# The convolution's banded product as 64x64 tiles on TensorE, its zero quarters left out, each half of the contraction in PSUM banks of its own

## The reference

```python
# first layer: per-batch mixing of the 64 channels, then a binary-weight product
x = x + _L0_ffn_ref(_L0_cond_ref(x, cond_128, ...), ...)
# second layer: a grouped convolution along the 1024 positions, then a product with W, Wq, Wk, A, Bm
def _L1_cond_ref(x, c, weight, c_weight, bias):
    C_OUT, K, GROUPS = (64, 9, 4)
    out = lax.conv_general_dilated(x, weight, window_strides=(1,), padding=[(4, 4)],
                                   dimension_numbers=('NCH', 'OIH', 'NCH'), feature_group_count=GROUPS)
    ctx = jnp.einsum('nd,od->no', c, c_weight)
    return out + ctx[:, :, None] + bias[None, :, None]
def _L1_ffn_ref(x, W, b, Wq, Wk, A, Bm):
    result = jnp.einsum('bsi,oi->bso', x, W) + b
    q, k = x @ Wq.T, x @ Wk.T                      # 8 experts of 32 each, here in short
    w = jax.nn.softmax((q * k).sum(-1) / math.sqrt(32), axis=-1)
    h = jnp.einsum('bsi,eri->bser', x, A)
    return result + jnp.einsum('bse,bser,eor->bso', w, h, Bm)
x = x + _L1_ffn_ref(_L1_cond_ref(x, cond_128, L1_cond_weight, L1_cond_c_weight, fside_S_0), L1_ffn_W, ...)
```

## Time and profile before

| what | value |
|---|---|
| median of 3 runs | 585.76 us (585.52 to 588.63) |
| the profiled execution | 585.94 us |
| its span | 584.2 us |
| TensorE, matmul records | 569.8 us busy (98% of the span), x3381 |
| VectorE | 232.6 us (40%) |
| ScalarE | 118.9 us (20%) |
| GpSimd | 148.1 us (25%) |
| DMA | 58.16 MB, mean 100 GB/s |
| chain that ended last | PE 94% |
| of it, line 473 (the convolution) | 10% |

### The profile page before, as it was taken

One profiled execution on the slowest core, in us unless ns is written; L12 is line 12 of the kernel. 1 busy time (PEld: TensorE's weight loads), 2 busy tenths in 40 slices (PEclk: granted clock), 3 DMA queues, 4 the chain that ended last, 5 costly groups with the idle time before them and its releaser, 6 DMA issues.

```text
span 584.2 us, 9131 instructions
## 1 busy us (share of the span) xinstructions
PE 569.8 (98%) x3381; PEld 502.3 (86%) x3381; DVE 232.6 (40%) x446; ACT 118.9 (20%) x271; POOL 148.1 (25%) x79
## 2 busy tenths in 40 slices
PE   4799999999999999999999999999999999999997
PEld 3688888888888899989989889899899898898996
DVE  3675677557765555221232232222312322222121
ACT  4732333324233341011111011011110110100100
POOL 0425636555456456101011011011010110110100
PEclk9889999999999999999999999999999999999999
DMA  8905324443253664303203123033032130230100
GB/s 327 356 34 162 117 78 132 135 119 117 76 175 100 158 165 123 111 3 113 90 24 112 45 67 112 33 79 103 9 112 75 37 112 36 76 111 8 67 37 36
DMA packets 36175, 58.16 MB, mean 100 GB/s; under 512 B 4097, under 2 KB 24385, under 8 KB 36161
## 3 DMA queue, kind: packets, MB, share of 16 engines
q1 hardware_dynamic: 36016, 57.70, 31.9%
q10 hardware_dynamic: 144, 0.26, 0.1%
HBM read 41.15 MB, written 16.79 MB: 99 GB/s over the span
## 4 chain that ended last, share of the span: by engine, by line
PE 94%; DVE 0%; issue 0%
PE bank L491 49%; PE bank L429 21%; PE bank L473 10%; PE bank L391 4%; PE bank L382 4%; PE bank L519 4%; PE bank L405 1%; PE bank L397 0%; PE bank L512 0%; PE bank L411 0%; DVE work L748 0%; DVE work L874 0%
## 5 line engine op out<-in xcount | busy, mean ns | idle before, releaser
L491 PE MATMUL bank<-early,parts 128*128 128x320 f32 (+1 forms) x1152 | 206.5, 337 | 0.0
L491 PEld LDWEIGHTS bank<-early,parts 128*128 128x128 f32 x1152 | 184.7, 188 | 15.7
L429 PE MATMUL bank<-late,parts 128*128 128x512 f32 x512 | 134.5, 411 | 1.5 <-ACT parts L609 1.5
L429 PEld LDWEIGHTS bank<-late,parts 128*128 128x128 f32 x512 | 93.5, 193 | 21.9 <-ACT parts L609 1.9
L931 POOL TENSOR_TENSOR work<-work,bias_bc 128x1024 f32<-128x1024 f32 x16 | 38.7, 2424 | 286.5 <-DMA work<-x_scratch 286.5
L491 PE MATMUL bank<-late,parts 128*128 128x512 f32 x384 | 94.2, 394 | 0.0
L491 PEld LDWEIGHTS bank<-late,parts 128*128 128x128 f32 x384 | 70.9, 188 | 16.1
L473 PE MATMUL bank<-band,raw 128*128 128x128 f32 x512 | 59.7, 275 | 0.0
L473 PEld LDWEIGHTS bank<-band,raw 128*128 128x128 f32 x512 | 59.0, 192 | 0.1
L609 ACT ACTIVATE parts<-work 128x512 fp32r<-128x512 f32 x64 | 39.8, 632 | 80.3 <-DVE work L823 43.0
L899 POOL TENSOR_TENSOR work<-work 128x512 f32<-128x512 f32 x32 | 41.3, 1291 | 52.5 <-DVE work L784 52.5
(11 more groups left out here) (88 smaller groups left out, 344.4 us busy)
## 6 DMA issues: line engine op xcount, KB each, us to landing
xs<-in_x SPq DMA_DIRECT2D x16, 512.0 KB, 3.9
x_scratch<-work SPq DMA_DIRECT2D x16, 512.0 KB, 3.0
raw<-x_scratch SPq DMA_DIRECT2D x128, 64.0 KB, 3.0
work<-x_scratch SPq DMA_DIRECT2D x16, 512.0 KB, 3.6
out_tokens<-work SPq DMA_DIRECT2D x15, 512.0 KB, 2.7
stage<-in_wearly SPq DMA_DIRECT2D x8, 576.0 KB, 3.8
row_bc<-token_rows_scratch SPq DMA_DIRECT2D x30, 64.0 KB, 3.6
work<-in_wsign SPq DMA_DIRECT2D x3, 512.0 KB, 11.3
```

What stands on the lines that cost most here:

```text
L429: last = mm(bank[4 + h][:, :], parts[:, p, a, c, :], signs[:, c, h * HALF:(h + 1) * HALF], start=(k % 16 == 0), stop=(k % 16 == 15))
L491: return mm(dst, parts[:, p, a, c, :], w(b, c), start=(k == 0), stop=(close and k == 23))
```

## The change

Each convolution is cut into products with 64 partitions of contraction and 64 stationary columns (64 output partitions). Of the four quarters of the band (half of the rows by half of the moving columns) one is zero in each step, and is left out: the low rows with s = 1 and the high rows with s = 0 meet all 128 moving columns, the low rows with s = 0 the first 64 alone, and the high rows with s = 1 the last 64 alone (`steps` below). The low rows add into banks 0 and 1, the high rows into two banks `other`: 2 and 3 for the first convolution, else those of the output of the tile whose turn is next. VectorE adds the two.

Since those banks are read by the sums of L874 (L897 in the new text), TensorE waits for `out_ready` before the convolution and not only before the period that writes them. The waits for `raw_loaded` and `out_ready` stand in front of the 37th of the 48 products.

```diff
-            def product_conv(i, p):
+            def inputs_of_conv(i, p):
                 pe.wait_ge(raw_loaded[p], (i + 1) * (16 * L8))
+
+            def product_conv(p, other):
+                low, high = slice(0, S), slice(S, P)
+                steps = ((low, 1, slice(0, P)), (high, 0, slice(0, P)), (low, 0, low), (high, 1, high))
                 for n in range(NBG):
-                    for s in range(2):
-                        last = mm(bank[n // 4][:, (n % 4) * P:(n % 4 + 1) * P], raw[:, p, n, s:s + P],
-                                  band[:, s * GROUPS + n % 4, :], start=(s == 0), stop=(s == 1))
-                    if n % 4 == 3:
-                        last.then_inc(conv_done, 1)
+                    for k, (rows, s, cols) in enumerate(steps):
+                        into = (bank[n // 4], bank[other + n // 4])[k % 2]
+                        at = (n % 4) * P
+                        for g in range(2):
+                            last = mm(into[g * S:(g + 1) * S, at + cols.start:at + cols.stop],
+                                      raw[rows, p, n, s + g * S:s + (g + 1) * S],
+                                      band[rows, s * GROUPS + n % 4, cols], start=(k < 2), stop=(k >= 2))
+                        if n % 4 == 3 and k >= 2:
+                            last.then_inc(conv_done, 1)
...
+                        if h == 1 and k == 12 and ni is not None:
+                            inputs_of_conv(ni, q)
+                            if late_ready:
+                                pe.wait_ge(out_scale_ready, 2 * TILES)
+                            else:
+                                pe.wait_ge(out_ready, 4 * i + 2 * p)
...
                 if ni is not None:
-                    product_conv(ni, q)
+                    product_conv(q, 4 + 2 * q)
...
-            def add_context(i, p, halves=(0, 1)):
+            def add_context(i, p, other, halves=(0, 1)):
...
-                    dve.wait_ge(conv_done, 4 * i + 2 * p + h + 1)
-                    v.tensor_tensor(zt, bank[h][:, :].rearrange("p (n l c) -> p n l c", n=4, l=L8),
-                                    add.broadcast_to([P, 4, L8, CG]), ALU.add).then_inc(z_biased, 1)
+                    dve.wait_ge(conv_done, 8 * i + 4 * p + 2 * h + 1)
+                    v.tensor_tensor(zt, by_group(bank[h]), add.broadcast_to([P, 4, L8, CG]),
+                                    ALU.add).then_inc(conv_halved, 1)
+                    dve.wait_ge(conv_done, 8 * i + 4 * p + 2 * h + 2)
+                    dve.wait_ge(conv_halved, 4 * i + 2 * p + h + 1)
+                    v.tensor_tensor(zt, by_group(bank[other + h]), zt, ALU.add).then_inc(z_biased, 1)
```

More of the change, by code:

```diff
@@ L187, in adaln_ffn_kernel @@
         conv_done = sem("conv_done")
+        conv_halved = sem("conv_halved")
         z_biased = sem("z_biased")
@@ L484, in _ @@
                     pe.wait_ge(pads_zeroed, 2)
-                    product_conv(0, 0)
+                    pe.wait_ge(u_ready, 2 * TILES)
+                    inputs_of_conv(0, 0)
+                    product_conv(0, 2)
                 ffn0_step(last_i, 1, k)
@@ L502, in period1 @@
                 if ni is not None:
-                    product_conv(ni, q)
+                    product_conv(q, 4 + 2 * q)
                 if late_ready:
                     pe.wait_ge(scaled, 2 * TILES)
-                    pe.wait_ge(out_scale_ready, 2 * TILES)
                 o = [bank[4 + 2 * p], bank[5 + 2 * p]]
@@ L812, in _ @@
             period0(last, 0, last, 1, False)
-            def add_context(i, p, halves=(0, 1)):
+            def add_context(i, p, other, halves=(0, 1)):
                 dve.wait_ge(ctx_loaded[p], 16 * (i + 1))
                 dve.wait_ge(z_lo, 4 * i + 2 * p)
+                by_group = lambda made: made[:, :].rearrange("p (n l c) -> p n l c", n=4, l=L8)
                 for h in halves:
-                    dve.wait_ge(conv_done, 4 * i + 2 * p + h + 1)
                     zt = y_t[:, :, 64 * h:64 * h + 64].rearrange("p l (n c) -> p n l c", c=CG)
                     add = row_bc[:, p:p + 1, 64 * h:64 * h + 64].rearrange("p l (n c) -> p n l c", c=CG)
-                    v.tensor_tensor(zt, bank[h][:, :].rearrange("p (n l c) -> p n l c", n=4, l=L8),
-                                    add.broadcast_to([P, 4, L8, CG]), ALU.add).then_inc(z_biased, 1)
+                    dve.wait_ge(conv_done, 8 * i + 4 * p + 2 * h + 1)
[4 more added lines that the diff above has]
+                    v.tensor_tensor(zt, by_group(bank[other + h]), zt, ALU.add).then_inc(z_biased, 1)
             dve.wait_ge(u_lo, 2 * TILES)
-            add_context(0, 0)
+            add_context(0, 0, 2)
             take_rest(0, 0, z_hi, z_lo, by_token)
@@ L861, in period1 @@
                 if ni is not None:
-                    add_context(ni, q, (0,))
+                    add_context(ni, q, 4 + 2 * q, (0,))
                 dve.wait_ge(wh_hi, t1)
@@ L867, in period1 @@
                     take_rest(ni, q, z_hi, z_lo, by_token, (0,))
-                    add_context(ni, q, (1,))
+                    add_context(ni, q, 4 + 2 * q, (1,))
                     take_rest(ni, q, z_hi, z_lo, by_token, (1,))
```

## The result

The change takes 578.89 us (median of 4 runs, 578.03 to 579.43) against 585.64 us for the kernel before on the same chip (585.13 to 588.63, 4 runs); the ratio is 0.9874, 95% interval 0.9844 to 0.9904. That is 1.0 to 1.6% faster. The forecast was 591.3 us, slower than before, and so had the wrong sign, though its wide range (576 to 612) holds the measured time. What was measured is near the first rival, four tiles by themselves (577 us).

What follows compares the result with a forecast made beforehand. TensorE's chain was taken as the bound: loads and streams 3.57 us plus entry and exit 0.35 make 3.92 against 3.57 us, +0.35 a convolution, x 16 = +5.6 us: 591.3 us. Range 576 to 612 us, the forecast's own 585 to 595.

Steps and rivals of the forecast that it cites:

- the first rival: Convolution: column halves load and stream independently, 3.02 us each, 8.8 us less in all, 577 us; chance 0.26.
- What bounds the kernel: Whole kernel: TensorE's gapless chain bounds it; the convolution's 16 x 3.57 = 57.1 us count fully in the time.
- The streams: Convolution: moving columns cost 0.334 us a block if four tiles run side by side, against 0.446 before.
- What runs side by side: TensorE: row groups run side by side and pass one another; for two column halves of one row group the trace shows nothing.
- The weight loads: Convolution: a row group's eight loads of 0.056 us go one behind another, 0.446 us a block, same as before.
- Entry and exit: Around each convolution: going from whole array to tiles and back costs 0.35 us, paid sixteen times.
- VectorE and the moved waits: VectorE's 22 us of added sums are hidden, and the moved waits for `out_ready` and `raw` cost nothing.
- The rival of strict order: Convolution: records keep program order over all tiles, 0.67 to 0.70 us a block, 620 to 624 us; shared chance 0.17.
- Column halves in line: Convolution: column halves run one after another, 5.7 us each, 34 us more in all, 620 us; shared chance 0.17.
- the middle variant: Convolution: tiles side by side but in order within a row group, 3.5 us, 585 to 586 us; chance within the forecast's 0.47.
- The sequencer: Convolution: issuing 128 records and loads is the bound if a pair costs over 0.028 us; with mixtures 596 to 612, chance 0.10.

Runs made afterwards that it cites:

- e7: The changed kernel with the convolution cut in two in the 15 second-stage periods, first four blocks behind the 37th of 48 products: 584.02 us, ratio 0.9936.
- e1: The changed kernel with the zero quarters multiplied too, so all eight products of a block have 128 moving columns: 591.95 us, ratio 1.0083.
- e3: The kernel before with only its stationary columns in two halves (128 rows, whole band, no second banks or sum): 590.27 us, ratio 1.0054.
- b1: The changed kernel with the first-stage router products' stationary columns also in two tiles of 64: 570.08 us in one execution.
- e8: The changed kernel without VectorE's second sum, leaving out half of the convolution's result: 579.41 us, ratio 0.9864.
- e5: The changed kernel reordered: in each convolution half all 32 records of the low rows, then the 32 of the high rows: 605.65 us, one execution.
- e6: The changed kernel reordered: in each convolution half all 32 records of the first 64 stationary columns, then the other 64: 605.44 us, one execution.
- the router's quarters: The changed kernel with the first-stage router products' stationary columns also in four tiles of 32: 571.27 us, ratio 0.9733.
- row halves alone: The changed kernel with row halves and zero quarters left out, but the stationary columns not halved: 592.38 us, ratio 1.0106.

## Why the prediction was wrong, step by step

**What bounds the kernel: right.** The chain is TensorE's, and the change moved the time by what it moved there. (The granted clock was full from the fourth slice on, not from the third; nothing hangs on it.)

**The streams: right.** 0.334 us a block for four tiles side by side were predicted, and 0.334 to 0.335 were measured (e7). The two terms are a little off in opposite ways: 0.112 and 0.055 us were taken for the wide and the narrow record, e1 gives (3.65 - 0.17)/32 = 0.109 for the wide one, which leaves 0.058 for the narrow one. That they cancel is luck.

**What runs side by side: half used.** The prediction read in the earlier trace rows that row groups pass one another, and left open whether two column halves in one row group do. They do, with whole rows (e3) as with half rows. The second record of a float32 product waits for its tile, but the other tiles' records pass it.

**The weight loads: the step that failed.** "If the two column halves of a row group load one behind the other, that is 8 x 0.056 = 0.446 us a block ... I take 0.446." They load side by side: in the change four loads begin together and the next four 0.06 us later, in e3 two and two, and a block takes 0.334 us. The price of a load was right (0.054 us for 64 columns by b1, 0.056 estimated), the number of them that queue was doubled. The choice went by line 391, which has one load after another because all of them are the whole array wide. It says what a load costs and nothing of how many go at once. The same trace had loads of two row groups side by side in line 405, at the same distance as one, and was as near a row. This step alone makes 0.90 us a convolution, 14.4 us: 591.3 less 14.4 is 576.9, against the measured 578.9.

**Entry and exit: right.** 0.35 us were predicted. The chain shows the way back by itself, 0.18 us; with a second entry (e7) it is 0.16 in and 0.20 back, 0.36 together. Of the streams' gain of 0.90 us a convolution this takes two fifths.

**VectorE and the moved waits: right.** Nothing for either (e8, and no wait of TensorE in the second stage).

**The rivals.** The first gave 3.02 us a convolution, 577 us; measured are 2.84 + 0.18 = 3.02 and 578.9 us. It had a chance of 0.26. The Trainium skill's page TensorEngine Tiling (Array Packing), section Key Properties of Tiling Modes, says the same of different tiles, that they can load and multiply in parallel; the four records and four loads that begin together agree. The rival of strict order falls by the same rows and by the some 7 records that TensorE passes over in e5 and e6. The Trainium skill's page TensorE: Matmul & The Clock Gate, Part 3, states that matmuls start and end strictly in program order, and that a load overlaps running matmuls only where its row group differs. This case's runs differ from both, and decide: a later record starts first in e5, and in e3 two loads begin within 0.02 us although all of them take all rows. The page speaks of a load beside a running matmul and not of two loads in a queue, so the forecast did not follow from it either. Column halves in line would have been 5.7 us a convolution, and the middle variant 3.5; both are far from 3.02. The sequencer isn't the bound at 0.021 us a record, the rate of the change: the router's quarters ran 64 records in 0.65 us, 0.010 each.

The sum for the change is 16 x 0.545 = 8.7 us; the medians differ by 6.75, and the interval of the ratio gives 5.6 to 9.1. In the profiled execution 1.5 us went in the first 40 us; why is not shown.

## What to carry to other kernels

A product that is smaller than the array, or whose matrix has zero blocks, can be cut into tiles that load and multiply at the same time, if entry and exit (0.36 us around the convolution) are paid once for many records and if the order in the code changes tiles within some eight records. Which cut pays depends on the limit: moving columns are saved by leaving out zero blocks, but only if the loads are halved too (row halves alone gained nothing), and a product that is limited by its loads gains by column tiles alone, without extra banks or sums. And a row that shows the price of one thing at a time doesn't say that two of them queue: where only that decides, give both cases equal weight and look for a row in which two were offered at once.

## What the runs showed of the hardware

- Four records, as many as there are tiles, began within 0.03 us, and each tile was limited by its own work: 0.109 us for a float32 record of 128 moving columns (e1), about 0.058 for 64 (the change, less that).
- A load cost about its width: 0.106 us for 128 columns, 0.054 for 64, 0.030 for 32 (with 8 moving columns, 0.17 us taken off for the entry to tiles), and loads of different column tiles went side by side.
- TensorE passed over some 6 to 8 waiting records to start one whose tile was free, across row halves and across column halves alike.
- From the whole array to tiles and back cost 0.36 us around the convolution, of which about half lay in the products behind; behind the router's column tiles these took only 0.08 us more.
- 64 loads and 64 matmuls were issued in 0.65 us, 0.010 us a pair. Whether issue or the array set that pace is not shown.
